# First sums table of a four-layer graph network: its bias rows written from a full tile on ScalarE's queue while the constants load

## The chip, the cores and the metric

The kernel runs on one core of one Trainium2 chip. The metric is device time in microseconds of that core, for one execution of the whole program, without the host. The engines are named as in the profile: PE (matmul), DVE (VectorE), ACT (ScalarE), POOL (GpSimd) and SP (SyncE). "ACTq" and "SPq" are what ACT and SP do in their instruction queues, the issue of DMAs among it.

## The reference

Four graph layers follow each other on 100000 nodes with 128 features and 50000 edges that are sorted by their destination. The first is a stack of three graph convolutions. What matters here is its first convolution:

```
def _gcn_conv(x, src, dst, ew, W, b):
    loop = jnp.arange(N, dtype=src.dtype)
    src2 = jnp.concatenate([src, loop])
    dst2 = jnp.concatenate([dst, loop])
    ew2 = jnp.concatenate([ew, jnp.ones((N,), dtype=ew.dtype)])
    deg = jax.ops.segment_sum(ew2, dst2, num_segments=N)
    dinv = jnp.where(deg > 0, jax.lax.rsqrt(jnp.maximum(deg, 1e-12)), 0.0)
    norm = dinv[src2] * ew2 * dinv[dst2]
    h = x @ W
    msg = norm[:, None] * h[src2]
    out = jax.ops.segment_sum(msg, dst2, num_segments=N)
    return out + b
```

The degree of a node is the sum of the weights of its incoming edges and one. After the three convolutions come a second layer with maxima and minima over edges, a third with means, and a fourth with attention, each with a layer norm behind it. All of them begin where the first has ended.

## The kernel before

The program is a row of stages, each with its own buffers and semaphores, and with a barrier of all five engines at its end (the method `__exit__` of `Phase`). Nodes are worked on in 98 chunks of 1024 nodes (the last has 672), in pairs; a chunk is a tile of 128 partitions with 8 nodes each. Edges are worked on in 49 chunks of 1024, also in pairs.

1. *Constants* (`load_constants`, from L158). SP issues the loads of all weights, biases and scales (L207). PE transposes ten weights, DVE copies them and computes a few rows. ACT has no part in this stage.
2. *Index tables* (`index_tables`). SP loads sources, destinations and weights of the edges (L278 to L284), DVE and PE turn them into tables, and SP writes three of them back to memory (L357, L358).
3. *Degrees* (`Degrees`, from L1841, and `degrees`, L2068). For each pair of edge chunks DVE adds the weights up along runs of equal destinations (L1974), PE turns the sums (L1961), DVE copies them to a slot (L1982), and POOL scatters them, in 8 indirect DMAs a chunk of 128 values of four bytes each, to the table `degree` (L1905). For each pair of node chunks SP loads the degrees (L1943) and x (L1950), DVE and ACT make the reciprocal root (ACT's square root at L2021 loads its table anew each time), both scale x by it (L2028 on ACT, L2060 and L2061 on DVE), and ACT stores the scaled rows (L2036).
4. The first convolution (`gcn_conv` with the name m0) and the rest.

Each convolution adds its messages into a table in memory, `sums_gcn0` for the first, which must hold the bias in each of its 100000 rows before the first message is scattered to it. The tables of the later convolutions are filled one stage ahead, on SP's queue (L1111). The first table is filled in the degree stage: behind the stores of each node pair ACT issues two more DMAs (L2040). Their source is the row of the bias, which stands in all partitions of `k["gcn_b0"]`, read eight times a partition by an access pattern with a stride of zero (`spread_slots`), so that each of the 8 nodes of a partition is a row of 512 bytes of its own. The loop is

```
for b in range(2):
    c = m * 2 + b
    n = sh.rows(c)
    act.dma_start(node_rows(self.fill_table, c, sh), spread_slots(self.fill_row[0:n, :], [n, T, D])).then_inc(self.filled, 16)
```

Edge and node work of the degree stage are merged by `merged_sweep`: every engine walks through the same units. In unit j it does its part of edge pair j and behind it its part of the node pairs from ready(j-1) to ready(j), a table made in the index stage that allows at most two node pairs a unit (`PACE`), in the first unit with nodes (the fourth) up to all that the pace has saved until then. An engine works strictly in this order. So DVE hands the next edge sums to POOL only when it is through with the node pairs ahead of them. Node work of a unit waits for the scatters of the unit two before it (SP waits for them, ahead of L1943). x, the scaled rows and the degrees have two buffers, one per chunk of a pair, so that the next pair's x is loaded when this pair's is scaled, and the next scaling waits until the store of the last one has landed.

Of the kernel before, what the change touches and what calls it, by code (L numbers as in the profile page):

```python
# [28 lines left out]
P = 128  # L29
D = 128  # L30
T = 8
# [123 lines left out]

def load_constants(nc, a, k):  # L158


    turned = {"pool1": a["L1_gnn_wpool1"], "self1": a["L1_gnn_wself1"], "eve1": a["L1_gnn_weve1"],
# [17 lines left out]
    with Phase(nc, "const") as ph:  # L179
        raw = {n: ph.sb(f"raw_{n}", [P, D]) for n in turned}  # L180
        relu_b = ph.sb("relu_b", [P, 2])
        relu_bm = ph.sb("relu_bm", [P, 2, P])
        att_cols = ph.sb("att_cols", [P, D])
        psum = [ph.ps(f"turn{i}", [P, 512]) for i in range(2)]
        eve_ps = ph.ps("eve", [P, 512])
        loaded = ph.sem("loaded")
# [15 lines left out]
        with nc.Block() as block:  # L202
            @block.sync
            def _(sp):
                sp.wait_ge(cleared, 7)
                for out, src in loads:
                    sp.dma_start(out, src).then_inc(loaded, 16)  # L207

            @block.gpsimd
            def _(pool):  # L210
# [1630 lines left out]
class Degrees(Phase):  # L1841
# [1 line left out]

    def __init__(self, nc, k, dram, sh, x, out, fill):
        super().__init__(nc, "deg")
        self.k, self.dram, self.sh, self.x_dram, self.out_dram = k, dram, sh, x, out
        self.fill_table, self.fill_row = fill

    def __enter__(self):
        super().__enter__()
        tiles = self.sh.edge_tiles
        self.pairs = [self.sb(f"pairs{b}", [2, 2 * CH]) for b in range(2)]
        self.sums = [self.sb(f"sums{b}", [2, CH]) for b in range(2)]
        self.both_tab = self.sb("both_tab", [P, tiles, 2])
        self.e_lift, self.e_pos, self.e_root, self.e_inv = (self.sb(n, [P, tiles]) for n in ("e_lift", "e_pos", "e_root", "e_inv"))
        self.deg_slot = [self.sb(f"deg_slot{b}", [P, T]) for b in range(4)]
        self.place_slot = [self.sb(f"place_slot{b}", [P, T], I32) for b in range(8)]
        self.sums_bank = [self.ps(f"sums_bank{b}", [P, T, 2]) for b in range(2)]  # L1860
        self.x = [self.sb(f"x{b}", [P, T, D]) for b in range(2)]
        self.xs = [self.sb(f"xs{b}", [P, T, WIDE]) for b in range(2)]
        self.deg, self.lift, self.pos, self.root, self.inv, self.dinv = (
            self.sb(n, [P, 2, T]) for n in ("deg", "lift", "pos", "root", "inv", "dinv"))
        self.gate = self.sem("gate")
        self.constants_set = self.sem("constants_set")
        self.mask_in, self.ew_in = self.pair("mask_in"), self.pair("ew_in")
        self.summed, self.turned = self.sem("summed"), self.sem("turned")
        self.deg_ready, self.counts_ready, self.place_set = self.sem("deg_ready"), self.sem("counts_ready"), self.sem("place_set")
        self.scattered = [self.sem(f"scattered{b}") for b in range(4)]  # L1870
        self.e_lifted, self.e_rooted, self.e_step = self.sem("e_lifted"), self.sem("e_rooted"), self.sem("e_step")
        self.x_in, self.deg_in, self.stored = self.pair("x_in"), self.pair("deg_in"), self.pair("stored")
        self.deg_read, self.lifted, self.rooted = self.sem("deg_read"), self.sem("lifted"), self.sem("rooted")
        self.inverted, self.dinv_ready = self.sem("inverted"), self.sem("dinv_ready")
        self.low_scaled, self.high_scaled = self.pair("low_scaled"), self.pair("high_scaled")
        self.filled = self.sem("filled")
        return self

    def grant(self, pool):
# [138 lines left out]
    def node_scalar(self, act, m, scattered):  # L2018
        sh = self.sh
        act.wait_ge(self.lifted, m + 1)  # L2020
        act.activation(self.root[:, :, :], self.lift[:, :, :], ACT.Sqrt).then_inc(self.rooted, 1)  # L2021
        act.wait_ge(self.dinv_ready, m + 1)
        for b in range(2):
            n = sh.rows(m * 2 + b)
            act.wait_ge(self.x_in[b], 16 * m + 16)
            act.wait_ge(self.stored[b], 16 * m + 16)
            for t in range(LOW):
                ins = act.activation(self.xs[b][0:n, t, 0:D], self.x[b][0:n, t, :], ACT.Copy, scale=self.dinv[0:n, b, t:t + 1])  # L2028
            ins.then_inc(self.low_scaled[b], 1)
        for b in range(2):  # L2030
            c = m * 2 + b
            act.wait_ge(self.low_scaled[b], m + 2)
            act.sem_inc(self.gate, 1)
            act.wait_ge(self.high_scaled[b], m + 2)
            act.sem_inc(self.gate, 1)
            act.dma_start(node_rows(self.out_dram, c, sh), self.xs[b][0:sh.rows(c), :, :]).then_inc(self.stored[b], 16)  # L2036
        for b in range(2):
            c = m * 2 + b
            n = sh.rows(c)
            act.dma_start(node_rows(self.fill_table, c, sh), spread_slots(self.fill_row[0:n, :], [n, T, D])).then_inc(self.filled, 16)  # L2040

    def node_vector(self, dve, m, scattered):
        sh, k = self.sh, self.k
# [21 lines left out]
            dve.tensor_tensor(k["dinv_sq"][:, column, :].rearrange("p o t -> p (o t)"), self.dinv[:, b, :], self.dinv[:, b, :], ALU.mult)  # L2065


def degrees(nc, k, dram, sh, x, out, fill):  # L2068
    with Degrees(nc, k, dram, sh, x, out, fill) as ph:
        with nc.Block() as block:  # L2070
            @block.gpsimd
            def _(pool):
                ph.grant(pool)
                ph.pool_program(pool)

            @block.sync
            def _(sp):
                sp.wait_ge(ph.constants_set, 4)
                merged_sweep(sp, k, sh, lambda *u: ph.sync(sp, *u), lambda *u: ph.load(sp, *u), first_behind=3)

            @block.tensor
            def _(pe):
                merged_sweep(pe, k, sh, lambda *u: ph.tensor(pe, *u), None)

            @block.scalar
            def _(act):
                act.wait_ge(ph.constants_set, 4)
                merged_sweep(act, k, sh, lambda *u: ph.scalar(act, *u), lambda *u: ph.node_scalar(act, *u), first_behind=3)
                for b in range(2):
                    act.wait_ge(ph.stored[b], 16 * sh.node_pairs + 16)  # L2090
                act.wait_ge(ph.filled, 16 * sh.node_chunks)

            @block.vector
            def _(dve):
                ph.vector_start(dve)
                dve.wait_ge(ph.constants_set, 4)
                merged_sweep(dve, k, sh, lambda *u: ph.vector(dve, *u), lambda *u: ph.node_vector(dve, *u), first_behind=3)
                dve.wait_ge(ph.e_step, 4)
# [393 lines left out]
def build(nc, a, out):  # L2492
# [17 lines left out]
    with ExitStack() as ctx:  # L2510
# [22 lines left out]
        for n in ("pool1", "self1", "eve1", "pool2", "self2", "eve2", "sage_l1", "sage_r1", "sage_l2", "sage_r2", "gcn0", "gcn1", "gcn2",  # L2533
                  "gcn_b0", "gcn_b1", "gcn_b2", "eve_b1", "eve_b2", "eve_r1", "eve_r2", "eve_c1", "eve_c2", "sage_b1", "sage_b2",
                  "gat_b", "bn_scale_row", "bn_shift_row"):
            keep(n, [P, D], stack=early)
        keep("zeros", [P, D + 1], stack=early)
        keep("bn_cols", [P, 2, D], stack=early)
        for n in ("ew_tab", "inv_count", "dinv_slot"):
            keep(n, [P, sh.edge_tiles], stack=early)  # L2540
        keep("dinv_sq", [P, sh.node_chunks, T], stack=early)

        load_constants(nc, a, k)
        index_tables(nc, a, k, dram, sh)
        def fill(n):
            return dram[f"sums_{n}"], k[bias_of[n]]

        x = a["x"]
        degrees(nc, k, dram, sh, x, dram["scaled_rows"], fill("gcn0"))

        gcn_conv(nc, k, dram, sh, "m0", 0, x, x, rows_a, None, k["bn1"], fill=fill("gcn1"))
        gcn_conv(nc, k, dram, sh, "m1", 1, rows_a, x, rows_b, k["bn1"], k["bn2"], fill=fill("gcn2"))
# [31 lines left out]
```

## Time and profile before

| | us |
|---|---|
| median of 3 runs | 11591.99 |
| lowest and highest run | 11556.57, 11599.9 |
| span of the profiled execution | 11581.2 |
| the profiled execution's own time | not given beside its span |
| constants stage | 0 to 43 |
| index stage | 43 to 88 |
| degree stage | 88 to 894 |
| everything behind it | 894 to 11581 |

The span is counted from the first to the last instruction of the profiled execution. The page says for each engine what share of the span it was busy: PE 53%, DVE 59%, ACT 40%, POOL 66%. DMAs are moved by 16 DMA engines that all queues share: q1 is SP's queue, q10 ACT's, q0 POOL's. Their share is the time in which packets were under way, as a mean over the 16 engines, so it counts a packet that is held up as busy too. The time between the issue of a DMA and its last byte is its time to landing. The stages' borders are read from the barriers.

### The profile page before, as it was taken

The page shows a single profiled execution, that of the slowest core. Times are in us where ns is not written, and L with a number is a line of the kernel's source. Part 1 is how long each engine was busy: PE and PEld are TensorE (multiplying, and loading weights), DVE is VectorE, ACT ScalarE, POOL GpSimd, SP SyncE. Part 2 cuts the span into 40 slices and gives each one's busy share as a digit, 9 for nine tenths or more (in the row PEclk, how much of TensorE's full clock was granted, in tenths as well). Part 3 has the DMA queues.
Part 4 walks back from the last instruction along what each step waited for, and adds up shares of the span by engine and source line. Part 5 has one row for each costly group of instructions (what it writes and reads, how often), then busy time and mean ns, then how long its engine had stood idle before and what let it go on. Part 6 is the DMA issues. An engine that isn't in the chain of part 4 may idle for free. (4 is left out here: it accounts for less than half of the span.)

```text
span 11581.2 us, 165045 instructions
## 1 busy us (share of the span) xinstructions
PE 6121.9 (53%) x35574; PEld 4955.3 (43%) x35575; DVE 6779.3 (59%) x16578; ACT 4593.8 (40%) x8654; POOL 7662.4 (66%) x7581
## 2 busy tenths in 40 slices
PE   1005666666566669865655554554454544444443
PEld 1005565566565653354444443544454422222221
DVE  3325555555555556555547775444466647777777
ACT  1111211222222225444435554333355546666665
POOL 4657776777677750177777775777777765666652
PEclk6557887788788889887877777777677766676675
DMA  5997777888788878676657776766688833333322
GB/s 140 223 192 230 260 253 232 283 296 302 250 290 301 297 260 285 224 244 239 226 199 270 259 256 201 256 240 241 216 313 285 291 107 106 110 102 111 110 96 79
DMA packets 1864913, 2570.41 MB, mean 222 GB/s; under 512 B 255773, under 2 KB 1369141, under 8 KB 1864662
## 3 DMA queue, kind: packets, MB, share of 16 engines
q1 hardware_dynamic: 1134168, 1627.27, 42.3%
q10 hardware_dynamic: 504726, 564.87, 14.9%
q0 software_dynamic: 225792, 375.94, 10.1%
q14 instruction: 169, 1.38, 0.0%
q8 instruction: 58, 0.95, 0.0%
HBM read 1499.62 MB, written 1129.98 MB: 227 GB/s over the span
## 5 line engine op out<-in xcount | busy, mean ns | idle before, releaser
L1128 PE MATMUL m_n_bank<-k_ident,m_in_y 128*128 128x128 f32 x5488 | 1009.4, 355 | 1549.2 <-DMA m_in_y<-node_rows_a 396.1
L1019 POOL DMA_INDIRECT sums_gcn<-m_result,m_idx x1176 | 1305.4, 1110 | 420.7 <-issue 348.6
L1128 PEld LDWEIGHTS m_n_bank<-k_ident,m_in_y 128*128 128x128 f32 x5488 | 865.9, 186 | 1648.7 <-issue 1067.6
L1011 POOL DMA_INDIRECT m_rows<-node_rows_a,m_idx x1176 | 1217.6, 1035 | 339.4 <-issue 335.2
L1154 ACT ACTIVATE m_nodeT<-m_n_bank 128x512 f32<-128x512 f32 x980 | 547.3, 597 | 1985.9 <-PE m_n_bank L1128 1973.0
L1019 POOL DMA_INDIRECT sums_eve<-m_result,m_idx x784 | 857.1, 1093 | 348.1 <-issue 231.9
L1019 POOL DMA_INDIRECT sums_sage<-m_result,m_idx x784 | 800.9, 1022 | 263.2 <-issue 230.7
L1011 POOL DMA_INDIRECT m_rows<-node_rows_b,m_idx x784 | 798.2, 1018 | 226.2 <-issue 225.2
L1060 PE MATMUL m_e_turn<-k_ident,m_rows 128*128 128x128 f32 x2744 | 529.5, 328 | 691.1 <-DVE m_sums L1529 327.0
L2181 POOL DMA_INDIRECT sums_gat<-g_result,g_idx x392 | 427.2, 1090 | 669.6 <-DVE g_result L2437 555.8
L1628 DVE SCALAR_TENSOR_TENSOR m_acc<-m_n_bank,m_scales,m_res_b 128x128 f32<-128x128 f32 (+1 forms) x2352 | 634.1, 342 | 264.7 <-PE m_n_bank L1139 204.3
L1060 PEld LDWEIGHTS m_e_turn<-k_ident,m_rows 128*128 128x128 f32 x2744 | 415.3, 173 | 816.4 <-DVE m_sums L1529 319.9
L1573 PE MATMUL m_gram<-m_y 128*128 128x129 f32 (+1 forms) x4800 | 613.1, 288 | 151.2 <-ACT m_y L1599 149.6
L743 ACT ACTIVATE m_o<-m_z,m_ln_shift,m_ln_scale 128x128 f32<-128x128 f32 x1600 | 626.4, 479 | 163.4 <-DMA node_rows_c<-m_o 105.4
L1905 POOL DMA_INDIRECT degree<-deg_deg_slot,deg_place_slot x392 | 452.0, 1153 | 327.4 <-DVE deg_deg_slot L1982 216.9
L1573 PEld LDWEIGHTS m_gram<-m_y 128*128 128x128 f32 (+1 forms) x4800 | 585.1, 201 | 174.8 <-ACT m_y L1599 173.4
L1615 DVE TENSOR_TENSOR m_res_b<-m_in_x,m_in_sums 128x1024 f32<-128x1024 f32 x196 | 240.2, 1226 | 648.0 <-DMA m_in_sums<-sums_gcn 646.5
L1156 ACT ACTIVATE m_nodeT<-m_n_bank,k_bn 128x512 f32<-128x512 f32 x392 | 285.5, 776 | 826.3 <-PE m_n_bank L1128 825.8
L1139 PE MATMUL m_n_bank<-k_gcn,m_nodeT 128*128 128x128 f32 (+1 forms) x4704 | 606.3, 285 | 0.0
L1070 PE MATMUL m_e_out<-k_gcn,m_sums 128*128 128x128 f32 x2352 | 417.3, 333 | 322.8 <-DVE m_result L1341 322.0
L1139 PEld LDWEIGHTS m_n_bank<-k_gcn,m_nodeT 128*128 128x128 f32 (+1 forms) x4704 | 586.8, 203 | 0.0
L998 POOL COPY m_idx<-k_edge_idx 128x16 int32 (+1 forms) x350 | 107.7, 310 | 715.9 <-POOLq L104 715.1
(295 smaller groups left out, 17377.3 us busy)
## 6 DMA issues: line engine op xcount, KB each, us to landing
m_in_sums<-sums_gcn SPq DMA_DIRECT2D x291, 512.0 KB
m_in_y<-node_rows_a SPq DMA_DIRECT2D x291, 512.0 KB
sums_gcn<-k_gcn_b SPq DMA_DIRECT2D x194, 512.0 KB
node_rows_a<-m_y ACTq DMA_DIRECT2D x194, 512.0 KB
m_in_x<-in_x_dram SPq DMA_DIRECT2D x194, 512.0 KB
m_in_y<-node_rows_b SPq DMA_DIRECT2D x194, 512.0 KB
sums_eve<-k_eve_b SPq DMA_DIRECT2D x194, 512.0 KB
m_in_sums<-sums_eve SPq DMA_DIRECT2D x194, 512.0 KB
```

The lines of the kernel that those rows point to most:

```text
L743: ins = act.activation(out[0:n, j, :], z[0:n, j, :], ACT.Identity, bias=self.shift[copy][0:n, at:at + 1], scale=self.scale[copy][0:n, at:a ...
L1011: pool.indirect_dma_start(self.rows[b][:, t, :], None, self.table[:, :], bass.IndirectOffsetOnAxis(self.idx[s][:, t:t + 1], 0)).then_inc(s ...
L1019: pool.indirect_dma_start(self.node_sums[:, :], bass.IndirectOffsetOnAxis(self.idx[s][:, T + t:T + t + 1], 0), self.result[b][:, t, :], No ...
L1060: mm = pe.transpose(bank[:, n * P:(n + 1) * P], self.rows[b][:, H * (i % 2) + n, 0:D], self.k["ident"][:, :])
L1070: mm = pe.matmul(bank[:, n * D:(n + 1) * D], lhs[:, n * P:(n + 1) * P], weight[:, :], start=True, stop=True)
L1128: mm = pe.transpose(self.n_bank[i][:, t * P:t * P + n], self.buf["y"][i // 2][0:n, H * (i % 2) + t, :], self.k["ident"][0:n, 0:n])
L1139: mm = pe.matmul(self.n_bank[i][0:n, t * D:(t + 1) * D], self.nodeT[:, i, t * P:t * P + n], weight[:, :], start=True, stop=True)
L1154: act.activation(out, src, ACT.Copy).then_inc(self.n_turn_read, 1)
L1573: mm = pe.matmul(self.gram[:, 0:D + 1], self.y1[b][0:rows[b], t, 0:D], self.y1[b][0:rows[b], t, :], start=False, stop=False, skip_group_ch ...
L1628: ins = dve.scalar_tensor_tensor(out=self.acc[b][0:n, tt, :], in0=ph.node_out(i, n)[:, t, :], scalar=self.scales[b][0:n, tt:tt + 1], in1=s ...
L1905: pool.indirect_dma_start(self.dram["degree"][:, :], bass.IndirectOffsetOnAxis(self.place_slot[s][:, t:t + 1], 0), self.deg_slot[b][:, t:t ...
L2181: pool.indirect_dma_start(self.node_sums[:, :], bass.IndirectOffsetOnAxis(self.idx[s][:, T + t:T + t + 1], 0), self.result[b][:, t, :], No ...
```

## The change

`load_constants` gets a block for ACT. It loads the bias row into all partitions, copies it eight times into a new tile `first_fill` of 128 x 8 x 128, and then issues the writes of all 98 chunks of the first sums table from this tile. The semaphore `first_filled` that they count up lives outside of the stages. The degree stage doesn't issue fills any more, and ACT waits for all 98 at its end.

```diff
-def load_constants(nc, a, k):
+def load_constants(nc, a, k, sh, first_sums, first_bias, first_filled):
...
+        first_row = ph.sb("first_row", [P, D])
+        first_in, first_made = ph.sem("first_in"), ph.sem("first_made")
...
+            @block.scalar
+            def _(act):
+
+                act.dma_start(first_row[:, :], first_bias.partition_broadcast(P)).then_inc(first_in, 16)
+                act.wait_ge(first_in, 16)
+                for t in range(T):
+                    ins = act.activation(k["first_fill"][:, t, :], first_row[:, :], ACT.Copy)
+                ins.then_inc(first_made, 1)
+                act.wait_ge(first_made, 1)
+                for c in range(sh.node_chunks):
+                    act.dma_start(node_rows(first_sums, c, sh), k["first_fill"][0:sh.rows(c), :, :]).then_inc(first_filled, 16)
...
-        self.filled = self.sem("filled")
...
-        for b in range(2):
-            c = m * 2 + b
-            n = sh.rows(c)
-            act.dma_start(node_rows(self.fill_table, c, sh), spread_slots(self.fill_row[0:n, :], [n, T, D])).then_inc(self.filled, 16)
...
-                act.wait_ge(ph.filled, 16 * sh.node_chunks)
+                act.wait_ge(first_filled, 16 * sh.node_chunks)
...
+        keep("first_fill", [P, T, D], stack=early)
...
-        load_constants(nc, a, k)
+        first_filled = nc.alloc_semaphore("first_filled")
+        load_constants(nc, a, k, sh, dram["sums_gcn0"], a["L0_gnn_bs"][0], first_filled)
```

ACT's listing shows the move. Before, its program begins with the first node pair of the degree stage (the names ahead of an arrow are what is written, those behind it what is read):

```order
L2021 ACTIVATE deg_root<-deg_lift 128x16
L2025 ISA
L2028 ACTIVATE deg_xs<-deg_x,deg_dinv 128x128 x4
L2032 REGISTER_ALU
L2036 ISA x2
L2036 DMA scaled_rows<-deg_xs 128x1056
L2036 ISA x2
L2036 DMA scaled_rows<-deg_xs 128x1056
L2040 ISA
L2040 DMA sums_gcn<-k_gcn_b 1024x1x128
L2040 ISA
L2040 DMA sums_gcn<-k_gcn_b 1024x1x128
```

The last four rows stand in every pair, and each fill has 1024 rows of 128 values. Now ACT's program begins in the constants stage:

```order
L214 DMA const_first_row<-in_L_gnn_bs_dram 128x128
L217 ACT_TABLE_LOAD
L217 ACTIVATE k_first_fill<-const_first_row 128x128 x8
L221 DMA sums_gcn<-k_first_fill 128x1024 x97
L221 DMA sums_gcn<-k_first_fill 84x1024
```

All 98 writes stand behind each other there, with 128 rows of 1024 values (the last 84), ahead of the stage's end. In the loop over pairs the rows of L2040 are gone, and nothing stands in their place.

## Rows read from the trace of the kernel before

**Rows 1.** Header of the page.

```profile
span 11581.2 us, 165045 instructions
```

**Rows 2.** Windows by stage: window and length, PE, PEld, DVE, ACT, POOL busy (x), clock, DMA share, GB/s.

```profile
0.00:43.00 43.00, 4.66 (x14) 2.69 (x15) 5.44 (x27) 0.02 (x1) 2.43 (x13) 1.00 0.21 44
43.00:88.00 45.00, 23.82 (x72) 16.23 (x72) 12.16 (x27) 0.00 (x0) 2.98 (x11) 1.00 0.14 37
88.00:160.00 72.00, 7.84 (x64) 7.38 (x64) 25.51 (x28) 1.50 (x2) 45.66 (x45) 0.50 0.10 22
160.00:212.00 52.00, 0.00 (x0) 0.00 (x0) 16.30 (x59) 15.80 (x34) 11.71 (x13) 0.50 1.01 318
212.00:563.00 351.00, 23.53 (x192) 22.16 (x192) 131.26 (x313) 69.03 (x144) 230.28 (x216) 0.50 0.97 228
563.00:894.00 331.00, 16.67 (x136) 15.70 (x136) 104.18 (x248) 55.03 (x115) 177.76 (x169) 0.50 0.96 193
```

**Rows 3.** Timeline of POOL, 321 to 350 us: start us, us, engine, line, instruction.

```profile
321.44 2.78 POOL L1905 DMA_INDIRECT degree<-deg_deg_slot,deg_place_slot  x1 [3.05 <-DVE deg_deg_slot L1982]
...
345.22 0.21 POOL L1891 COPY deg_place_slot<-k_edge_idx 128x8 int32 x1
350.05 2.91 POOL L1905 DMA_INDIRECT degree<-deg_deg_slot,deg_place_slot  x1 [4.62 <-DVE deg_deg_slot L1982]
```

**Rows 4.** Waits of POOL (total us, times, longest), 212 to 563, then 563 to 900 us.

```profile
POOL degree L1905 <- DVE deg_deg_slot L1982: 95.4, 11, 37.8
...
POOL degree L1905 <- DVE deg_deg_slot L1982: 106.7, 10, 16.8
```

**Rows 5.** Windows inside the degree stage: two with few or no scatters, one full of them.

```profile
184.00:212.00 28.00, 0.00 (x0) 0.00 (x0) 9.66 (x37) 9.34 (x20) 0.00 (x0) 0.50 1.07 369
700.00:706.00 6.00, 1.86 (x16) 1.83 (x16) 4.81 (x4) 0.00 (x0) 5.02 (x3) 0.50 1.05 391
711.00:729.00 18.00, 0.00 (x0) 0.00 (x0) 2.00 (x8) 2.48 (x5) 10.85 (x12) 0.50 0.96 160
```

**Rows 6.** Timeline of ACT and its queue, 710 to 729 us.

```profile
710.19 1.28 ACTq L2036 DMA_DIRECT2D scaled_rows<-deg_xs  x2
711.63 6.26 ACTq L2040 DMA_DIRECT2D sums_gcn<-k_gcn_b  x2
718.24 1.28 ACT L2021 ACT_TABLE_LOAD   x1 [8.06 <-issue]
...
728.71 0.69 ACT L2028 ACTIVATE deg_xs<-deg_x,deg_dinv 128x128 f32<-128x128 f32 x2 [5.64 <-DMA scaled_rows<-deg_xs]
```

**Rows 7.** DMA issues of 88 to 160 and of 563 to 894 us, median us to landing last.

```profile
degree<-deg_deg_slot,deg_place_slot POOLq DMA_INDIRECT x38, 2.2
...
degree<-deg_deg_slot,deg_place_slot POOLq DMA_INDIRECT x152, 12.5
```

**Rows 8.** Lines L2040 and L2036 on ACT's queue, ns min/median/max.

```profile
L2040 ACTq DMA_DIRECT2D sums_gcn<-k_gcn_b x98: 564/1076/7562, 164.7 to 892.1; - x98
...
L2036 ACTq DMA_DIRECT2D scaled_rows<-deg_xs x98: 337/344/716, 163.3 to 890.8; - x98
```

**Rows 9.** Timeline of ACT and its queue, 221 to 228 us, from an empty queue.

```profile
221.01 1.28 ACT L2028 ACTIVATE deg_xs<-deg_x,deg_dinv 128x128 f32<-128x128 f32 x4 [0.86 <-DVE deg_dinv L2054]
222.31 1.25 ACTq L2036 DMA_DIRECT2D scaled_rows<-deg_xs  x2
223.73 4.51 ACTq L2040 DMA_DIRECT2D sums_gcn<-k_gcn_b  x2
```

**Rows 10.** DMA queue q10 (ACT's), 222.2 to 228.24 us: packets, MB, share of 16 engines.

```profile
q10 hardware_dynamic: 146, 0.56, 23.6%
```

**Rows 11.** Timeline of the index stage from its start, 43 to 54 us.

```profile
43.52 0.53 POOL L327 MEMSET index_int_src<- 128x512 int32 x1 [40.31 <-POOLq L104]
...
52.13 0.25 SPq L284 DMA_DIRECT2D index_flt_ew<-in_edge_weight_dram  x1
...
53.58 0.43 DVE L370 CAST index_flt_src<-index_int_src 128x512 f32<-128x512 int32 x1 [11.01 <-DMA index_flt_ew<-in_edge_weight_dram]
```

More of the change, by code:

```diff
@@ L1841, with __init__ @@
 class Degrees(Phase):
-    def __init__(self, nc, k, dram, sh, x, out, fill):
+    def __init__(self, nc, k, dram, sh, x, out):
         super().__init__(nc, "deg")
         self.k, self.dram, self.sh, self.x_dram, self.out_dram = k, dram, sh, x, out
-        self.fill_table, self.fill_row = fill
     def __enter__(self):
@@ L2065, in node_vector, with degrees @@
             dve.tensor_tensor(k["dinv_sq"][:, column, :].rearrange("p o t -> p (o t)"), self.dinv[:, b, :], self.dinv[:, b, :], ALU.mult)
-def degrees(nc, k, dram, sh, x, out, fill):
-    with Degrees(nc, k, dram, sh, x, out, fill) as ph:
+def degrees(nc, k, dram, sh, x, out, first_filled):
+    with Degrees(nc, k, dram, sh, x, out) as ph:
         with nc.Block() as block:
@@ L2548, in build @@
         x = a["x"]
-        degrees(nc, k, dram, sh, x, dram["scaled_rows"], fill("gcn0"))
+        degrees(nc, k, dram, sh, x, dram["scaled_rows"], first_filled)
         gcn_conv(nc, k, dram, sh, "m0", 0, x, x, rows_a, None, k["bn1"], fill=fill("gcn1"))
```

## The prediction, made before the changed kernel ran

> **What bounds the kernel now.** The page's header gives the span, 11581.2 us [rows 1]; the page holds no other time of that execution. The sum below is made against this span, which lies 10.8 us under the median of the runs, 11591.99, and I add its result to the median. Then I read the windows by stage [rows 2]. The constants take 43 us and the index tables 45, both at a DMA share of 0.14 to 0.21. The degree stage runs from 88 to 894 us, and from 160 us on its DMA share is 0.96 to 1.01. That looks like a stage bound by the DMA engines, so the question is what the bytes cost in it.
>
> They don't cost the same everywhere. The rate is 318 GB/s in 160 to 212 us, then 228, then 193, at the same share [rows 2]. Inside the stage [rows 5], 28 us without one scatter run at 369 GB/s and 6 us around a first scatter at 391, while 18 us with 12 scatters run at 160. So the four-byte scatters of the degrees slow all traffic beside them, and the engines count as busy meanwhile. The scatters themselves land after 2.2 us in the quiet part and after 12.5 us in the late part [rows 7].
>
> The second bound is POOL. A unit of two edge chunks begins its scatters at 321.44, is through at 345.4, and then waits 4.6 us for DVE to hand over the next chunk [rows 3]. Its own work is thus 24.0 us a unit. DVE comes late because it does two node pairs in between. POOL waits 95.4 us for it up to 563 us, of which 37.8 are one wait that ends at 212 us after a burst of five pairs, and 106.7 us after 563 [rows 4]. Those waits are what a lighter DMA load can win. A late pair shows its chain [rows 6]: two stores are issued at 710.19, two fills block ACT's queue for 6.26 us, the square root's table load comes only at 718.24, and the next scaling waits at last for the store issued 18 us earlier, until 728.71.
>
> **The change, part by part.** The 98 fills of 512 KB leave the degree stage.
>
> *What the degree stage wins.* Two go with each of 49 pairs: five pairs stand in 160 to 212 us, and of the other 88 fills I put 48 before 563 us and 40 behind it, by the length of the two stretches and their rates. In bytes that is 5.2, 25.2 and 20.8 MB. Priced at the rate without scatters, 369 GB/s, they take 14, 68 and 56 us. Priced at their stretches' own rates they take 16, 110 and 108. In the middle stretch no more than POOL's waits can go, 95.4 - 37.8 = 57.6 us, since then POOL's 24.0 us a unit bind. In the late stretch the like bound is 106.7. The fast rate gives 14 + 57.6 + 56 = 128 us, the slow ones 16 + 57.6 + 106.7 = 180. I take 128. A store waits for stalled traffic, not only for the fills behind it, so the fills should be worth what they take in the fast moments. The lowest I can argue is 14 + 0 + 56 = 70 us, if in the middle another wait of DVE takes the place at once. ACT's blocked time (the fill's issue has a median of 1.08 us and a maximum of 7.6 [rows 8]) lies inside these figures. So does the final wait: it is for fills that landed hundreds of microseconds before, and costs nothing.
>
> *What the start pays.* The new block on ACT loads one row (some 3 us, an estimate), loads a table (1.28 us, the length in [rows 6]), makes eight copies at 0.32 us (four 128x128 in 1.28 us [rows 9]) and then issues 98 writes, the first at about 8 us. Nothing on ACT waits for them, but the stage ends with a barrier that ACT must reach too, so the 98 issues must be through. Here the decisive rows are [rows 8 to 10]. A store of 128 rows issues in 0.34 us. From an empty queue, two stores and two fills (2 x 128 + 2 x 1024 = 2304 rows) don't go out at once: the fills take 4.51 us where twice the minimum of 0.56 would do, and when they are through, the queue has started 146 packets. So about 2304 - 146 = 2158 rows can lie in the queue, and the next issue stands still. Rows of 512 bytes or of 4 KB should count alike, as stores and fills lie mixed there. The new writes have 128 rows each: 17 lie in the queue, and the others go out only as it drains.
>
> Draining 51.2 MB at 369 GB/s takes 139 us, and the constants' own 1.9 MB (44 GB/s over 43 us [rows 2]) some 5 more. The last write lands at 8 + 139 + 5 = 152 us, the last one is issued 17 x 1.42 = 24 us earlier, at 128. The index stage, which began at 43.5 [rows 11], would begin at 129: **86 us later**. PE's and DVE's work on the constants (until 43) lies under this. The index stage's loads are then issued while 24 us of fill are still moving. They landed 1.2 us after the last issue [rows 11]; sharing every engine with 4 KB packets may double their 10 us, and I add 8 (0 to 14). The rest of the stage is a chain of PE and DVE and stays. So the degree stage starts 94 us later. At 391 GB/s and no loss in the index stage it would be 80; at 318 GB/s (the stretch from 160 to 212) 8 + 161 + 6 - 28 = 147 us, so 104 + 10 = 114.
>
> A rule of the Trainium skill gives another drain. Its page "DMA: Bandwidth & Descriptors", section Specifications, puts HBM at about 358 GB/s per core. By that rule the drain would be an estimated 143 us and the sum below -31 instead of -34; [rows 5] show 369 and 391, so the trace doesn't keep to it, though only part of that traffic is writes.
>
> Other edits cost nothing: the fill tile is 4 KB a partition, the broadcast bias row on SP stays, and SP, PE, DVE and POOL keep their orders. From the barrier at 894 us on nothing moves.
>
> *Sum.* +94 - 128 = **-34 us**, 11547 against the span and 11558 against the median. It is a large exchange that nearly cancels: bytes leave a stage in which they ride beside other work, and come to one in which nothing else runs and everyone waits for them. About 0.5% (58 us) is what a measurement of this kernel can tell from no change, since its three runs spread by 43 us.
>
> **The rivals.**
> *A, ACT isn't held.* If the limit is not one of rows, the 98 issues go out at 0.34 to 0.63 us each (the store's issue, and half of the pair's 1.25 us [rows 9]), some 49 us, and the barrier comes at 57 us, 14 later. The index stage runs wholly beside the fill, +15. Then +29 - 128 = -99 us, 11493. Against it stand [rows 9, 10]. The same page of the Trainium skill, section "Issuing engines are not separate DMA queues", says that initiating DMAs takes a sequencer time that is usually small beside the DMA itself. By that rule this rival would hold.
> *B, POOL's floor is reached.* Without fills DVE is always in time, and the waits go wholly: 14 + 57.6 + 106.7 = 178 us. Sum 94 - 178 = -84, 11508. For it: the waits follow the load, 3 to 5 us early and up to 16.8 late. Against it: the stall by scatters grew over the stage and stays, with two thirds of the bytes.
> *C, the chain stays.* The middle of the stage wins nothing, 70 us in all: +24, 11616. For it: the scaling waits for stores that lie beside stalled traffic [rows 6].
> *D, slower: the writes alone are slow.* No row shows a stretch of writes alone. If they go at the late stretch's 193 GB/s, the fill takes 265 us, the last issue comes at 278 - 46 = 232 us, and the start is 189 + 8 = 197 us late: +69, 11661. It ends slower than before from a shift of 128 us on, which is a fill of 181 us or 282 GB/s, and beyond 0.5% from about 203 GB/s down. Against it: 369 GB/s at two thirds writes [rows 5].
> *That the change isn't there* is excluded: the listing of ACT shows the 98 writes ahead of the stage's end and none in the loop.
>
> **How the numbers follow.** My forecast has 0.60, A 0.08, B 0.13, C 0.12, D 0.07. The range of 11490 to 11625 (-102 to +33) takes in A, B, C and most of the bounds of the two unknown costs (80 - 180 = -100 and 114 - 70 = +44), and leaves out D and the ends. Faster by over 0.5%: A, B and 0.09 of my own case's lower part, 0.30. Slower by over 0.5%: D and a rest, 0.08. Within: 0.62.
>
> **What would show it.** The index stage's first memset at about 129 us; a queue of ACT whose issues cost 0.34 us at first and then about 1.4; a degree stage of about 678 us instead of 806, with POOL's waits for DVE below 100 us in all; the rate with scatters still at 160 to 200 GB/s. I am wrong if the first memset comes before 70 us (A) or after 160 (D), or if the degree stage stays above 740 us (C) or falls to 630 (B).

## The result and the profile after

| | before | after |
|---|---|---|
| median of 18 runs each, us | 11589.5 | 11617.22 |
| lowest and highest, us | 11555.47, 11608.58 | 11606.58, 11650.67 |
| ratio of the two, 95% interval | | 1.0027 (1.002 to 1.0034) |
| span of the profiled execution, us | 11581.2 | 11615.1 |
| constants stage, until / length | 43.0 / 43.0 | 129.9 / 129.9 |
| index stage | 87.7 / 44.6 | 180.1 / 50.3 |
| degree stage | 897.6 / 809.9 | 919.0 / 738.9 |
| everything behind it, length | 10682.7 | 10695.1 |

The kernel became 27.7 us slower, 0.24%: within the half per cent, but on the other side of the forecast of -34, and at the place of rival C (11616). The lengths are read from the barriers of the profiled executions. The degree stage of before ends at 897.6 us and not at 894 as given ahead of the prediction, so it is 810 us long and not 806. The start costs 92.4 us, the degree stage wins 71.0. The 12.4 us behind it are not the change's, as far as the runs tell: the same stages took 10675 to 10709 us in the twelve profiled executions of this study, in no order that follows the fills.

The header and the windows of after, with the columns of [rows 2]:

```profile
span 11615.1 us, 164863 instructions
...
0.00:130.00 130.00, 4.67 (x14) 2.69 (x15) 5.45 (x27) 3.00 (x10) 2.43 (x13) 1.00 0.96 378
50.00:73.00 23.00, 0.00 (x0) 0.00 (x0) 0.00 (x0) 0.00 (x0) 0.00 (x0) 1.00 0.85 313
73.00:129.00 56.00, 4.67 (x14) 2.68 (x14) 5.43 (x26) 0.00 (x0) 0.00 (x0) 1.00 1.03 420
130.00:180.00 50.00, 24.56 (x72) 16.43 (x72) 12.17 (x27) 0.00 (x0) 2.98 (x11) 1.00 0.33 116
252.00:300.00 48.00, 0.00 (x0) 0.00 (x0) 16.84 (x59) 15.81 (x34) 10.98 (x13) 1.00 0.75 241
300.00:600.00 300.00, 23.57 (x192) 22.21 (x192) 124.51 (x294) 64.77 (x134) 227.40 (x207) 1.00 0.66 173
600.00:919.00 319.00, 16.68 (x136) 15.71 (x136) 109.53 (x266) 59.43 (x125) 189.80 (x178) 1.00 0.74 145
```

The constants stage, quiet before at a share of 0.21, is now full of writes; alone they go at 420 GB/s. The degree stage is no longer full (0.66 to 0.74 against 0.96 to 0.97), yet its rate stays low. The granted clock of TensorE was at its lower level there in before (0.50, 1.2 GHz) and at its upper one in after (1.00, 2.4 GHz). It explains none of the difference: the same 192 matmuls kept PE busy for 23.53 us in before [rows 2] and 23.57 in after, and the other kernels below show long and short degree stages at either level. The timeline of the constants stage of after (ACT and its queue, PE's first instruction, POOL's first one of the index stage), and PE's first in before:

```profile
3.79 1.70 ACT L217 ACTIVATE k_first_fill<-const_first_row 128x128 f32<-128x128 f32 x8 [1.34 <-DMA const_first_row<-in_L_gnn_bs_dram]
5.53 30.50 ACTq L221 DMA_DIRECT2D sums_gcn<-k_first_fill  x25
...
74.60 0.47 PE L246 MATMUL const_turn<-k_ident,const_raw_pool 128*128 128x128 f32 x1 [74.60 <-DMA k_bconv<-in_L_gnn_bconv_dram]
...
130.36 0.52 POOL L341 MEMSET index_int_src<- 128x512 int32 x1 [127.15 <-POOLq L104]
```

```profile
33.69 0.47 PE L232 MATMUL const_turn<-k_ident,const_raw_pool 128*128 128x128 f32 x1 [33.69 <-DMA k_bconv<-in_L_gnn_bconv_dram]
```

The issues of the writes on ACT's queue, and of one kind of load on SP's queue (ns min/median/max), of after, and that load in before:

```profile
L221 ACTq DMA_DIRECT2D sums_gcn<-k_first_fill x98: 352/1228/3042, 5.5 to 128.0; - x98
...
L209 SPq DMA_DIRECT2D k_gat_e<-in_L_gnn_We_dram x8: 1211/1250/1322, 14.1 to 23.2; - x8
```

```profile
L207 SPq DMA_DIRECT2D k_gat_e<-in_L_gnn_We_dram x8: 420/420/429, 9.5 to 12.8; - x8
```

ACT is held until 129.5, as forecast. Beside that the writes slow the stage's own loads: SP's small DMAs (8 KB each in the rows above) issue in 1.25 us where 0.42 was enough, and PE, which waits for the last of them, begins at 74.6 instead of 33.7.

In the degree stage POOL's waits and the chain through the stores are what to read. Waits (us in total, times, longest) of the whole stage, 180 to 925 us of after, and of before from 88 to 900:

```profile
ACT deg_xs L2040 <- DMA scaled_rows<-deg_xs: 235.5, 53, 9.4
DVE deg_xs L2068 <- DMA scaled_rows<-deg_xs: 208.9, 53, 8.9
...
POOL degree L1917 <- DVE deg_deg_slot L1994: 141.1, 16, 34.2
...
DVE deg_inv L2057 <- ACT deg_root L2033: 36.4, 47, 2.3
```

```profile
POOL degree L1905 <- DVE deg_deg_slot L1982: 216.9, 22, 37.8
...
DVE deg_inv L2049 <- ACT deg_root L2021: 153.2, 49, 9.2
ACT deg_xs L2028 <- DMA scaled_rows<-deg_xs: 121.7, 38, 6.1
...
DVE deg_xs L2060 <- DMA scaled_rows<-deg_xs: 105.1, 37, 5.7
```

DVE no longer waits for the square root behind ACT's blocked issues (153.2 down to 36.4), but it and ACT now wait twice as long for the store of the last pair to land (105.1 up to 208.9 and 121.7 up to 235.5). Most of the removed wait came back in the same chain. POOL's waits fell by 76 us, close to the 71 us that the stage won. A late piece of ACT's timeline, the counterpart of [rows 6], and then the DMA issues from 600 to 919 us (median us to landing last), to [rows 7]:

```profile
784.14 1.28 ACT L2033 ACT_TABLE_LOAD   x1 [1.69 <-issue]
787.80 0.21 ACT L2033 ACTIVATE deg_root<-deg_lift 128x16 f32<-128x16 f32 x1 [2.38 <-DVE deg_lift L2054]
790.62 0.69 ACT L2040 ACTIVATE deg_xs<-deg_x,deg_dinv 128x128 f32<-128x128 f32 x2 [2.61 <-DMA scaled_rows<-deg_xs]
797.60 0.69 ACT L2040 ACTIVATE deg_xs<-deg_x,deg_dinv 128x128 f32<-128x128 f32 x2 [6.29 <-DMA scaled_rows<-deg_xs]
```

```profile
degree<-deg_deg_slot,deg_place_slot POOLq DMA_INDIRECT x160, 10.7
```

No fill is in the queue, and the stores issued at 782 still land only at 797. The scatters take 10.7 us, hardly less than the 12.5 of [rows 7].

The starts of POOL's units divide the win (units are counted from 1). Unit 4 is the first behind the burst of nodes, and unit 16 begins at 563 us in before. POOL's timeline at these two, of before and of after:

```profile
212.38 2.67 POOL L1905 DMA_INDIRECT degree<-deg_deg_slot,deg_place_slot  x1 [37.76 <-DVE deg_deg_slot L1982]
...
563.16 2.78 POOL L1905 DMA_INDIRECT degree<-deg_deg_slot,deg_place_slot  x1 [7.90 <-DVE deg_deg_slot L1982]
```

```profile
300.14 2.67 POOL L1917 DMA_INDIRECT degree<-deg_deg_slot,deg_place_slot  x1 [34.25 <-DVE deg_deg_slot L1994]
...
620.05 2.77 POOL L1917 DMA_INDIRECT degree<-deg_deg_slot,deg_place_slot  x1 [9.70 <-DVE deg_deg_slot L1994]
```

From the stage's start to unit 4: 124.7 before, 120.0 after, a win of 4.6. From unit 4 to unit 16: 350.8 and 319.9, a win of 30.9. From there to the end: 334.4 and 299.0, a win of 35.5 (rounded; together 71.0). The prediction had 14, 57.6 and 56.

### The profile page after: what moved, and what is told of

It is laid out like the page before. It is cut to its first block and busy times, and to the rows that moved or that the text cites. A ratio compares the mean times of both kernels' runs of the same rounds, so it can differ in the third digit from the quotient of the medians.

```text
span 11615.1 us, 164863 instructions
## 1 busy us (share of the span) xinstructions
PE 6112.6 (53%) x35574; PEld 4947.3 (43%) x35575; DVE 6774.1 (58%) x16578; ACT 4598.9 (40%) x8663; POOL 7706.9 (66%) x7581
## 5 line engine op out<-in xcount | busy, mean ns | idle before, releaser
L1587 PEld LDWEIGHTS m_gram<-m_y 128*128 128x128 f32 (+1 forms) x4800 | 593.7, 204 | 181.8 <-ACT m_y L1613 180.1
L1917 POOL DMA_INDIRECT degree<-deg_deg_slot,deg_place_slot x392 | 459.2, 1172 | 251.1 <-DVE deg_deg_slot L1994 141.1
L1746 DVE TENSOR_TENSOR m_z<-m_n_bank,m_in_sums 128x512 f32<-128x512 f32 x392 | 254.3, 686 | 543.6 <-ACT m_o L1788 174.9
```

Of the source, the lines that this page charges most:

```text
L1587: mm = pe.matmul(self.gram[:, 0:D + 1], self.y1[b][0:rows[b], t, 0:D], self.y1[b][0:rows[b], t, :], start=False, stop=False, skip_group_ch ...
L1917: pool.indirect_dma_start(self.dram["degree"][:, :], bass.IndirectOffsetOnAxis(self.place_slot[s][:, t:t + 1], 0), self.deg_slot[b][:, t:t ...
```

## The experiments

Two questions were open. What of the 92 us at the start is ACT's hold at the barrier, and can the writes stand where they hold nobody? And why are the fills worth 71 us in the degree stage: by their bytes, by their form (1024 rows of 512 bytes), by two at a time on ACT's queue, or only because the scatters stall what lies beside them? All diffs are against the changed kernel unless they say otherwise. Ratios are against before, measured beside each group of kernels (medians 11589.9, 11590.14 and 11590.92).

| kernel | median us (runs) | ratio, interval | start until | degree stage |
|---|---|---|---|---|
| half | 11585.61 (10) | 0.9997 (0.9988 to 1.0007) | 130.1 | 758.3 |
| deg_start | 11599.73 (10) | 1.0008 (0.9997 to 1.0018) | 86.9 | 815.9 |
| split | 11554.78 (6) | 0.9971 (0.9956 to 0.9987) | 93.6 | 771.1 |
| small_rows | 11677.16 (4) | 1.0068 (1.0048 to 1.0088) | 235.9 | 742.3 |
| packed_loop | 11593.37 (10) | 1.0006 (0.9996 to 1.0015) | 88.7 | 825.5 |
| spread | 11580.72 (10) | 0.9991 (0.9981 to 1.0) | 89.2 | 805.9 |
| after_dropped | 11502.47 (1) | one run | 181.5 | 642.4 |
| before_dropped | 11431.12 (1) | one run | 89.0 | 649.1 |
| wide_table | 11437.08 (4) | 0.9864 (0.9847 to 0.988) | 87.0 | 654.6 |
| split_wide | 11478.02 (4) | 0.9898 (0.9882 to 0.9915) | 108.9 | 666.5 |

"Start until" is the end of the index stage, us. The lengths of a degree stage are those of one profiled execution each.

### half: 49 writes in the constants, 49 at the start of the degree stage

```diff
-                for c in range(sh.node_chunks):
+                for c in range(49):
...
+                for c in range(49, sh.node_chunks):
+                    act.dma_start(node_rows(first_sums, c, sh), k["first_fill"][0:sh.rows(c), :, :]).then_inc(first_filled, 16)
                 act.wait_ge(ph.constants_set, 4)
```

> 49 of the 98 writes stay in the constants stage, 49 are issued by ACT at the start of the degree stage, where it has nothing to do for 62 us. Theory 1 (the barrier is held by ACT's issues at 1.27 us each): ACT is through at 68 us, so what holds the constants stage is then the slowed loads of SP, which ended PE's and DVE's work at about 83 us in the changed kernel; first memset of the index stage at 84 us, degree stage near 739 us, time about 11617 - 46 = 11571 us. Rival (the loads' contention alone holds the stage, ACT's issues don't): the memset at 129 us as before, no gain, 11617 us.

ACT's queue, timeline:

```profile
5.40 61.43 ACTq L221 DMA_DIRECT2D sums_gcn<-k_first_fill  x49
...
130.63 63.68 ACTq L2097 DMA_DIRECT2D sums_gcn<-k_first_fill  x49
```

The constants end at 84.7 instead of 129.9. ACT is through at 66.8, so here it isn't ACT that the barrier waits for: PE begins at 75.3, because SP's loads land as late as with 98 writes. So of the 87 us the change adds to this stage, some 42 come from the slowed loads and the other 45 from ACT's hold. The degree stage, expected at 739 us, takes 758.3 and so gives back 19 of the microseconds won, for ACT is busy with issues until 194.3 and the burst of node pairs can't begin.

### deg_start: all 98 writes at the start of the degree stage

The loop over 98 chunks leaves `load_constants` and stands ahead of `act.wait_ge(ph.constants_set, 4)` in `degrees`.

> All 98 writes are issued by ACT at the start of the degree stage; the tile is still made in the constants stage. Theory 1: constants and index stage as in the kernel before (43 and 45 us); ACT is held until about 88 + 125 = 213 us, while its first node pair was due at 158, so the degree stage is about 739 + 55 = 794 us long and the time 11589 - 71 + 55 = 11573 us. Rival (fills beside scatters cost as much there as in the loop): degree stage 810 us or more, 11589 us.

```profile
87.40 139.30 ACTq L2095 DMA_DIRECT2D sums_gcn<-k_first_fill  x98
...
233.16 3.41 ACTq L2046 DMA_DIRECT2D scaled_rows<-deg_xs  x2
```

POOL's unit 4:

```profile
281.08 2.67 POOL L1915 DMA_INDIRECT degree<-deg_deg_slot,deg_place_slot  x1 [105.43 <-DVE deg_deg_slot L1992]
```

The start is back at 86.9, which shows that nothing else in the change delays it. Each issue now takes 1.42 us beside the index reads and the first scatters, where 1.27 did in the constants. ACT makes its first store at 233 instead of 163 [rows 8]. These 70 us are lost for the burst of five node pairs (55 were expected), and the stage is no shorter than in before. Its 815.9 us are what the rival expected, but not for the rival's reason. From unit 4 on, deg_start takes 622 us (281.08 to 902.8), nearly the 619 of after and far from the 685 of before. The whole loss lies ahead of unit 4.

### split: 8 writes behind the loads, 26 in the index stage, 64 in the degree stage

```diff
+                act.wait_ge(loaded, 16 * len(loads))
+                for c in range(8):
...
+            @block.scalar
+            def _(act):
+                act.wait_ge(loaded, n_loaded[0])
+                for c in range(8, 34):
...
+                for c in range(34, sh.node_chunks):
                 act.wait_ge(ph.constants_set, 4)
```

> 8 writes in the constants stage once its loads have landed, 26 in the index stage once its loads have landed, 64 at the start of the degree stage. Theory 1: constants at most 3 us longer, index stage 3 to 5 us longer, ACT free at 88 + 8 + 64 x 1.27 = 177 us against 158 when its first pair is due, so degree stage 739 + 19 = 758 us, time 11589 - 71 + 19 + 6 = 11543 us. If the writes disturb the scatters of the first units: 11560 us or more. Rival (no placement helps, since the bytes cost the same everywhere): 11589 us.

```profile
34.60 7.97 ACTq L222 DMA_DIRECT2D sums_gcn<-k_first_fill  x8
54.55 31.66 ACTq L386 DMA_DIRECT2D sums_gcn<-k_first_fill  x26
...
94.16 99.33 ACTq L2105 DMA_DIRECT2D sums_gcn<-k_first_fill  x64
```

Placed behind each stage's own loads, 34 writes cost the start 6 us in all (93.6 against 87.7). The 64 others take 1.55 us each beside scatters and hold ACT until 193.5. It is 35 us under before's median and the only placement of the writes alone with an interval wholly below 1; 12 us of what was expected are missing, since 1.55 us an issue is more than the constants stage showed.

### small_rows: the same 98 writes from one row read eight times

Only slot 0 of `first_fill` is made, and the source is `spread_slots(k["first_fill"][0:sh.rows(c), 0, :], [sh.rows(c), T, D])`.

> The changed kernel with rows of 512 bytes: the tile holds one row, read eight times, and 98 fills of 1024 rows are issued in the constants stage. Theory 1 (issues go at the pace of the drain): a fill of 512 KB in rows of 512 bytes took 1.5 us at 346 GB/s, so the issues end at 8 + 98 x 1.5 = 155 us less about 2, first memset at 153, time 11617 + 24 = 11641 us. Rival (the number of rows that fits into the queue sets the hold, my sum's step): about the same memset, but SP's loads, which alternate with shorter packets, end earlier than 73 us. Rival (the eight copies and the 4 KB rows are what the change gains): no difference in the degree stage, which would say they gain nothing.

Its window from 10 to 190 us:

```profile
10.00:190.00 180.00, 4.67 (x14) 2.68 (x14) 5.42 (x26) 0.00 (x0) 0.00 (x0) 1.00 1.01 281
```

ACT's queue, and PE's first instruction:

```profile
3.99 185.91 ACTq L219 DMA_DIRECT2D sums_gcn<-k_first_fill  x98
63.80 0.47 PE L244 MATMUL const_turn<-k_ident,const_raw_pool 128*128 128x128 f32 x1 [63.80 <-DMA k_bconv<-in_L_gnn_bconv_dram]
```

The same bytes in rows of 512 bytes go at 281 GB/s against 393 in after from 10 to 129 us. An issue takes 1.9 us and not the 1.5 that was expected. In the constants the full tile is thus worth 60 us (190.3 against 129.9) where 24 were expected. SP's loads end earlier than in after, as the first rival said. The degree stage (742.3) is that of after.

### packed_loop: before's order, with fills from the full tile

```diff
-                for c in range(sh.node_chunks):
-                    act.dma_start(node_rows(first_sums, c, sh), k["first_fill"][0:sh.rows(c), :, :]).then_inc(first_filled, 16)
...
+        for b in range(2):
+            c = m * 2 + b
+            act.dma_start(node_rows(self.dram["sums_gcn0"], c, sh), self.k["first_fill"][0:sh.rows(c), :, :]).then_inc(self.first_filled, 16)
```

> The fills stay in the loop over node pairs, where the kernel before has them, but read 4 KB rows from the tile. The kernel with rows of 512 bytes at the start took 185.9 us for 98 writes where 4 KB rows took 123.9, so a write is 0.63 us cheaper and the loop moves 62 us less of DMA time. Theory 2 (what the degree stage wins is DMA time of the fills): about a third of the 71 us comes from the form of the rows alone, degree stage 785 us, time 11565 us. Rival (the chain through the landing store binds, and fills ride beside it): the stage stays above 800 us. Second rival (ACT's blocked issues made it late; they fall from 1024 rows to 128): the stage falls to 750 us.

Missed. The rows that cost 60 us in the constants cost nothing in the degree stage: 825.5 against 809.9, and the total is before's. Waits of the whole stage, 88 to 920 us:

```profile
POOL degree L1915 <- DVE deg_deg_slot L1992: 226.9, 23, 38.4
...
ACT deg_xs L2038 <- DMA scaled_rows<-deg_xs: 190.1, 48, 9.7
...
DVE deg_inv L2058 <- ACT deg_root L2031: 72.6, 48, 4.9
```

The wait for the square root halves (153.2 to 72.6) and the one for the stores grows (121.7 to 190.1). It is the same exchange as in after. The form of a fill isn't what binds.

### spread: 8 writes behind the loads, 20 in the index stage, 21 at the start of the degree stage, 49 in the loop, one a pair

> 8 writes behind the loads of the constants stage, 20 behind those of the index stage, 21 at the start of the degree stage, and one with each of 49 node pairs, all in 4 KB rows. Theory 1: nobody waits for ACT any more: constants 43.5 us, index stage 45 to 47, first node pair at its old time. The loop carries a quarter of the DMA time of the old fills (49 x 1.27 of 98 x 1.9 would be a third). If half of the 71 us that the fill-free stage wins is kept with them: degree stage 770 us, time 11555 us; if the light fills ride for nothing: 745 us, 11525 us. Rival (a fill in the loop costs as much as its share of ACT's waits, whatever its form): 11575 us.

Waits of the stage, 88 to 900 us:

```profile
ACT deg_xs L2048 <- DMA scaled_rows<-deg_xs: 251.2, 50, 11.8
...
POOL degree L1925 <- DVE deg_deg_slot L2002: 215.4, 22, 36.2
```

Missed: 770 us or less were expected by the theory. The start costs next to nothing (89.2), and half of the fills are out of the loop, but the stage takes 805.9 us. POOL waits as long as in before. A fill of 512 KB per pair costs nearly as much as two. So the win isn't in proportion to the bytes, which was the ground of the prediction's 14, 68 and 56. Why one fill a pair costs nearly as much as two isn't shown.

### after_dropped and before_dropped: the scatters write nothing

```diff
-        nodes_end = pool.to_reg(sh.n - 1)
+        nodes_end = pool.to_reg(0)
```

All values for nodes other than node 0 lie outside of the bound and aren't written. The 392 indirect DMAs are issued as before, and the degrees stay unsummed.

> The changed kernel with the bounds of the degree scatter set to 0, so POOL issues all of them, but the values for other nodes than node 0 are dropped and no degree arrives in the table. Theory 3 (the landing of the four-byte values stalls all DMAs, and the chain of a pair waits for stalled stores): the rate in the loop is no longer bound by stalls, the store lands in 4 to 5 us, and POOL waits for DVE only behind the first burst: degree stage 739 - 73 - 30 = 640 us. Rival (the chain is long by itself, table load, handshakes and order): 720 us or more.

> The kernel before with the same edit: scatters issued, values dropped. Theory 3: without stalls a pair moves its 3.1 MB in 8.5 us, two pairs in 17, less than POOL's 24 us a unit, so the fills ride for nothing and the degree stage is about as long as in the changed kernel with the same edit, 640 to 655 us. Rival (fills cost their DMA time in any case): 70 us more than there.

Windows of before_dropped, to the last two of [rows 2]:

```profile
212.00:563.00 351.00, 29.45 (x240) 27.70 (x240) 156.13 (x377) 83.29 (x175) 283.10 (x266) 1.00 0.85 277
563.00:738.00 175.00, 10.80 (x88) 10.17 (x88) 73.94 (x180) 40.28 (x85) 128.58 (x120) 1.00 0.82 264
```

This is the main finding. Without the values, the 98 fills cost 6.7 us (649.1 against 642.4, one execution each); with them 71.0. The written values cost 161 us beside the fills (809.9 against 649.1) and 96 without them (738.9 against 642.4). The rate stays at 264 to 277 GB/s with all the fills in it, where before had 228 and 193. Rival B expected a win of 178 us in this stage, and something near it (161 to 168) comes only with the stall gone.

The single packets show the stall as well. Those of the loads of x (4096 bytes) take 159 ns in the median behind the burst in before, in after and in before_dropped. On the mean they take 313 ns in before and 328 in after, where 7% of them need over 1 us, but 200 ns in before_dropped, where 1% do. So taking the fills out left the stall of a packet about as it was, and took away packets that would wait in it.

### wide_table: before, with the degrees 64 bytes apart

Against before:

```diff
-            "degree": scratch("degree", [nodes_padded, 1]).ap(),
+            "degree": scratch("degree", [nodes_padded * 16, 1]).ap(),
...
+        dve.tensor_scalar(self.places[:, :, :], self.k["edge_idx"][:, :, 1, :], 16.0, None, ALU.mult).then_inc(self.placed, 1)
...
-        nodes_end = pool.to_reg(sh.n - 1)
+        nodes_end = pool.to_reg((sh.n - 1) * 16)
...
-        dve.tensor_scalar(self.lift[:, :, :], self.deg[:, :, :], 1.0, 1e-12, ALU.add, ALU.max).then_inc(self.lifted, 1)
+        dve.tensor_scalar(self.lift[:, :, :], self.deg_wide[:, :, :, 0], 1.0, 1e-12, ALU.add, ALU.max).then_inc(self.lifted, 1)
```

The table is cleared by 16 DMAs instead of one, and SP loads it with 512 bytes a partition. The fills stay in the loop.

> The kernel before with one change of another kind: the table of degrees has its values 64 bytes apart (16 words a node, cleared whole, 6.4 MB), so two neighbouring nodes no longer share 64 bytes; places are multiplied by 16, the degree loads are 512 bytes a partition and DVE reads every sixteenth word. Fills stay in the loop. Theory 3a (the stall comes from values that fall next to each other): stalls vanish, degree stage towards the 649 us of the run with dropped values plus some microseconds, say 660, index stage 0 to 10 us longer, time 11440 us. Rival 3b (any four-byte value written costs the same stall, wherever it falls): the stage stays at 810 us, time 11590 us or more.

Its windows, to the last two of [rows 2], and its waits from 87 to 745 us:

```profile
212.00:563.00 351.00, 28.45 (x233) 26.78 (x232) 155.44 (x377) 83.29 (x174) 282.61 (x262) 0.50 0.88 283
563.00:741.00 178.00, 10.80 (x88) 10.17 (x88) 74.64 (x180) 40.84 (x85) 131.18 (x123) 0.50 0.85 275
```

```profile
POOL degree L1920 <- DVE deg_deg_slot L1998: 52.3, 5, 35.0
...
ACT deg_xs L2045 <- DMA scaled_rows<-deg_xs: 3.7, 5, 1.4
```

As many values of four bytes are written as in before, by the same DMAs, with the words of neighbouring nodes 64 bytes apart instead of four. The stage falls to 654.6 us, within 6 us of the kernel that writes none, the wait for stores from 121.7 to 3.7, and POOL's wait from 216.9 to 52.3, of which 35.0 are the burst. The kernel is 154 us faster than before and 180 faster than after. It is the best of the study. The 4096-byte packets take 208 ns on the mean, as without the values.

More than the distance changed with it. The table takes 6.4 MB instead of 0.4, and a load of the degrees of one chunk moves 64 KB instead of 4. The small loads alone don't make the stall, since before_dropped has them too and doesn't stall. But whether the values disturb each other, or disturb the loads from the same stretch of the table, or gain by being spread over more memory, these runs can't tell apart.

### split_wide: both

> The split kernel (8 writes in the constants stage, 26 in the index stage, 64 at the degree stage's start) with the same wide table. Theory 3a: without stalls fills in the loop cost nothing, and the 64 at the start still hold ACT to about 175 us, so this gives about the time of the wide table alone, 11440 to 11450 us. Rival 3b: its own 11555 us or more.

Missed: 41 us slower than wide_table. The index stage takes 65.6 us. The clearing of the table alone left it at 42.9 (wide_table) and the 26 writes alone at 49.7 (split), so it is the two together. In the degree stage ACT is held to 195 us by the other 64 writes, and POOL has one wait of 53.1. ACT's queue, and the waits from 108 to 776 us:

```profile
54.05 39.69 ACTq L398 DMA_DIRECT2D sums_gcn<-k_first_fill  x26
109.45 85.81 ACTq L2122 DMA_DIRECT2D sums_gcn<-k_first_fill  x64
```

```profile
POOL degree L1940 <- DVE deg_deg_slot L2018: 70.6, 2, 53.1
```

With the stall gone there is little left to win by moving fills (6.7 us between the two dropped kernels), and their issue in a block costs more than that.

## Why the prediction was right and wrong

**The constants, +86: measured +86.9.** The end of ACT's issues, put at 128, came at 129.5. But two of the working's three steps were wrong and cancelled. *The limit of 2158 rows* in ACT's queue doesn't hold for these writes. By it 17 would have gone out at once. In fact seven had gone out by 12 us, and 25 took 30.5 us. At 130 us, 378 GB/s x 130 us = 49.1 MB had moved, 1.9 of them the constants', so 47.2 of 51.2 MB of writes: about 8 were outstanding at the last issue, not 17. Issues went at the pace of the drain almost from the beginning. In small_rows, 50.4 MB had moved on ACT's queue at 190 us, so less than two fills were outstanding, which are about 1660 of its rows against the 1000 rows of the 8 here. What sets the depth isn't settled; one count of rows doesn't fit both. *The drain* was put at 369 GB/s, and was 392 to 420 but for the stretch from 50 to 73 us. A shallower queue made the last issue later, a faster drain made it earlier, by about the same. The 358 GB/s of the Trainium skill ("DMA: Bandwidth & Descriptors", Specifications) was further off still. The Trainium skill's page "HBM Reference", Specifications (TRN2), says that a core streaming alone reaches about 425, and the 420 GB/s from 73 to 129 us agree with that.

**What the prediction didn't see there:** SP's issues and loads. It said that PE's and DVE's work on the constants lies under the hold. It did, but with some 45 us to spare and not 86, since PE could begin only 41 us later. That made no difference to the time of this kernel, but it limits every repair: half won 45 us in the constants stage, not 87. Rival A, with issues at 0.34 to 0.63 us, was wrong: the median is 1.23. With all engines busy an issue took as long as the DMA's share of the drain (512 KB at 420 GB/s are 1.25 us). The Trainium skill's rule that the sequencer time of initiating a DMA is usually small beside the DMA itself ("DMA: Bandwidth & Descriptors", Issuing engines are not separate DMA queues) doesn't hold for these writes.

**The index stage, +8: measured +5.7.** Within the range given (0 to 14). The reason given, that its loads are issued beside the last writes, fits half, where the writes are through before it and it takes 45.4 us.

**The degree stage, -128: measured -71.0. This step failed**, and with it the sign. It priced the fills by their bytes at the rate without scatters, and let POOL's waits go wholly in the middle. Measured were 4.6, 30.9 and 35.5 us for 14, 57.6 and 56. The argument of rival C, that the scaling waits for stores beside stalled traffic, was the right one. The wait for stores rose from 121.7 to 235.5 us on ACT as the one for the square root went. C had the middle at zero and the rest whole. In truth every stretch won between a third and two thirds of the forecast, so that C's 70 meets 71 by the sum and not by its parts. packed_loop and spread show that neither the form of the fills nor half of their number matters. The two dropped kernels show that without the written values all of the 71 us but 6.7 are gone, and wide_table that the layout of the table decides it, with the words of neighbouring nodes 4 or 64 bytes apart. Rival B's floor isn't reached, as POOL still waits 141.1 us. The prediction had named this stall ("slow all traffic beside them"), and then treated it as fixed and the fills as the cost. What stays open is how fills and stall add up: the values cost 161 us with the fills beside them and 96 without, and half of the fills cost nearly as much as all.

**Rival D** fell (420 GB/s, not 193), though with rows of 512 bytes, as before's fills have them, the rate of 281 put the start 148 us late and the total at 11677 (small_rows). The final wait cost nothing, as predicted: the last write was issued 789 us before the degree stage ends.

**The sum:** 92.4 - 71.0 = +21.4 by the stages, +27.7 by the medians; the rest lies in the scatter of what comes behind.

## What to carry to other kernels

A stage whose DMA share is near 1 but whose rate falls to half need not be bound by its bytes. Taking bytes out of this one gave back 71 us where 128 were priced. Find what stalls the engines, here by dropping the suspected values in one run. Bulk writes in a quiet stage aren't free: they hold the issuing engine at the stage's barrier and slow the issues and loads of the other queue, so put them behind the stage's own loads and only as many as drain before the stage would end. Where large transfers ride beside small scattered values, try the table with its words further apart: at 64 bytes this stage fell from 809.9 to 654.6 us.

## What was not expected of the hardware

- Four-byte scatters into a table with its words side by side slow the large transfers beside them: 228 and 193 GB/s at shares of 0.97 and 0.96, against 283 and 275 when the words are 64 bytes apart. The Trainium skill's page "DMA: Bandwidth & Descriptors", Specifications, says that transfers under 512 bytes are written by reading and modifying. Spans of 512 bytes hold the words of 128 nodes in before and of 8 in wide_table, so these runs don't tell whether a span of 512 bytes, of 64 or of another size is what collides. Distances other than 4 and 64 bytes weren't tried, and how the stall comes about isn't shown.
- Writes of 512 KB with rows of 4 KB reached 420 GB/s alone and 393 with the constants' loads beside them, with rows of 512 bytes 281. The same page gives 512 bytes as the least size for the full rate; the trace doesn't agree. Beside scatters the degree stage was no shorter with rows of 4 KB (825.5 against 809.9 us).
- With the engines saturated by one queue, an 8 KB load of the other took 1.25 us to issue instead of 0.42. With small_rows, at a lower rate, PE could begin its work at 63.8 us, earlier than at 74.6. How two queues share the engines by packets or rows wasn't followed up.
